# Attention beside an FP4 gated layer on one core: gate, up and down weights handled in portions within the projections, and the main stage's constants and first loads placed in the maximum stage

## The reference

```python
xn = _layernorm(x, axis=-1)
x = x + _L0_attn_ref(xn, Wqkv, Wout, bout) + _L0_ffn_ref(xn, w_gate, w_up, w_down)

# attention: 16 heads of 16, causal
qkv = xn @ Wqkv.T
attn = softmax(where(causal_mask, -inf, q k^T * dh ** -0.5))
out = (attn v) @ Wout.T + bout

# gated layer, width 704; fp4_linear quantises both operands
# in blocks of 16: scale = max|block| / 6, values on a grid of 8
h = silu(fp4_linear(xn, w_gate)) * fp4_linear(xn, w_up)
y = fp4_linear(h, w_down)
```

## Time and profile before

| | |
|---|---|
| median of 3 runs | 2537.82 us (2537.43 to 2541.84) |
| profiled execution | 2539.19 us, span 2537.5 us |
| PE busy | 2314.7 us, 91% |
| DVE busy | 2038.4 us, 80% |
| ACT busy | 1952.0 us, 77% |
| POOL busy | 645.4 us, 25% |
| granted clock of PE, mean | 0.975 of full speed |

### The profile page before, as it was taken

One profiled execution on the slowest core, in us unless ns is written; L12 is line 12 of the kernel. 1 busy time (PEld: TensorE's weight loads), 2 busy tenths in 40 slices (PEclk: granted clock), 3 DMA queues, 4 the chain that ended last, 5 costly groups with the idle time before them and its releaser, 6 DMA issues.

```text
span 2537.5 us, 86209 instructions
## 1 busy us (share of the span) xinstructions
PE 2314.7 (91%) x34104; PEld 1273.9 (50%) x34104; DVE 2038.4 (80%) x5932; ACT 1952.0 (77%) x3342; POOL 645.4 (25%) x524
## 2 busy tenths in 40 slices
PE   2895999999999993999999999999999999999998
PEld 1784444444444441455555555555555555555555
DVE  7674999999999994787777777777777777787775
ACT  1342999999999992888878788878788877788875
POOL 3111343333344322222221222221221221212221
PEclk7898999999999996999999999999999999999999
DMA  2575455545555532111021011021011021011000
GB/s 52 188 225 151 66 76 76 76 71 69 71 69 76 76 52 71 23 31 29 15 68 37 27 40 29 15 68 37 28 40 29 15 68 37 28 39 29 15 21 31
DMA packets 94537, 143.82 MB, mean 57 GB/s; under 512 B 24896, under 2 KB 73920, under 8 KB 93632
## 3 DMA queue, kind: packets, MB, share of 16 engines
q1 hardware_dynamic: 89792, 129.50, 26.1%
q0 software_dynamic: 4352, 8.92, 1.4%
HBM read 104.20 MB, written 34.14 MB: 55 GB/s over the span
## 4 chain that ended last, share of the span: by engine, by line
PE 47%; ACT 7%; issue 5%; DVE 3%; DMA 0%; SPq 0%; POOL 0%; DVEq 0%; ACTq 0%; POOLq 0%
PE O L1051 16%; PE F L1072 10%; PE S L1030 9%; ACT probs L1181 6%; PE F L1109 5%; PE F L1118 2%; PE F L1098 2%; PE S L1036 1%; DVE o_turned L1402 0%; ACT xt_hi L1186 0%; DVE o_turned L1403 0%; PE S L1118 0%; DMA v_in<-s_v 0%; DVE o_sum L1407 0%; DVE xt_lo L1352 0%
## 5 line engine op out<-in xcount | busy, mean ns | idle before, releaser
L1181 ACT ACTIVATE probs<-S 128x1024 f32<-128x1024 f32 (+3 forms) x1280 | 1082.7, 896 | 309.5 <-PE S L1036 184.9
L775 ACT ACTIVATE m_excess<-m_DIFF 128x512 f32<-128x512 f32 (+7 forms) x1536 | 646.8, 472 | 85.7 <-PE m_DIFF L735 40.1
L793 DVE CUSTOM_DVE_ANT_0 m_excess<-m_S,m_excess 128x512 f32<-128x512 f32 (+7 forms) x1536 | 700.6, 530 | 11.7 <-PE m_S L735 9.6
L1051 PE MATMUL O<-probs,v_sb 64*32 64x512 f32 (+3 forms) x10240 | 614.3, 533 | 1.0 <-ACT probs L1181 1.0
L733 PE MATMUL m_S<-m_k,m_q 128*128 128x512 f16 (+7 forms) x1536 | 482.6, 324 | 26.7 <-DVE m_row_max L793 17.4
L733 PE MATMUL m_DIFF<-m_k,m_q_diff 128*128 128x512 f16 (+7 forms) x1536 | 477.6, 318 | 26.6 <-DMA m_q_diff<-s_q 26.3
L1030 PE MATMUL S<-q_st,k_st 64*32 64x512 f16 (+3 forms) x10240 | 414.9, 350 | 82.7 <-ACT probs L1181 43.8
L1030 PEld LDWEIGHTS S<-q_st,k_st 64*32 64x32 f16 x10240 | 148.9, 90 | 412.7 <-ACT probs L1181 251.4
L677 POOL TENSOR_TENSOR m_q_diff<-m_zero,m_q 48x4096 f16<-48x4096 f16 x32 | 224.4, 7011 | 428.8 <-DMA m_q<-s_q 418.1
L733 PEld LDWEIGHTS m_S<-m_k,m_q 128*128 128x128 f16 x1536 | 148.1, 96 | 276.1 <-DVE m_row_max L793 195.5
L735 PE MATMUL m_S<-m_future,m_ident 128*128 128x64 bf16 x1024 | 197.1, 193 | 0.0
(11 more groups left out here) (183 smaller groups left out, 3966.6 us busy)
## 6 DMA issues: line engine op xcount, KB each, us to landing
m_q<-s_q SPq DMA_DIRECT2D x96, 128.0 KB, 3.8
m_k<-s_k SPq DMA_DIRECT2D x96, 128.0 KB, 6.8
m_q_diff<-s_q SPq DMA_DIRECT2D x96, 128.0 KB, 8.1
k_st<-s_k SPq DMA_DIRECT2D x96, 128.0 KB, 4.3
q_st<-s_q SPq DMA_DIRECT2D x384, 32.0 KB
m_k<-s_k SPq DMA_DIRECT2D x96, 124.0 KB, 5.3
a_x<-in_L_attn_x_dram POOLq DMA_DIRECT2D x16, 512.0 KB, 4.8
s_q<-a_part SPq DMA_DIRECT2D x32, 256.0 KB, 2.5
```

Source lines behind the costliest of these rows:

```text
L775: act.activation(excess[u % MAX_EXCESS][:, 0:keys // 2], DIFF[u % MAX_BUFS][:, 0:keys // 2], ACT.Relu) \
L793: dve.tensor_tensor_reduce(larger, S[u % MAX_BUFS][:, 0:keys // 2], larger, 1.0, -3e38, ALU.add, ALU.max, column).then_inc(reduced[u % MAX ...
L1051: ins = pe.matmul(O[e][s * SLOT:(s + 1) * SLOT, st.skip:QC], v_sb[st.group % 2][rows, st.j, s * SLOT:(s + 1) * SLOT], probs[s // 2][st.n % ...
L1181: act.activation(probs[half][st.n % PROBS][:, :, 0:st.width], S[half][:, :, 0:st.width], ACT.Exp, scale=scale).then_inc(exped[half], 1)
```

## The change

The quantisation of the three matrices leaves weights_phase. Their buffers and steps are in a class GatedWeights; weights_phase clears the buffers and issues their loads behind those of Wqkv and Wout. The 16 projection groups are written out without a loop, and at the end of some of them DVE does a portion: all of `scales`, the exponent and step of the rounding, its add, or its subtraction. POOL's `normalise` and `rescale` follow in the same groups. After the last group come the 12 fills, in the banks of the projections. The buffers, constants and first loads of main_phase go to a class Ahead: POOL writes the constants after the first two negations of the maximum stage and places v at its end, SP issues the first loads after the last stacks. The split and store of the last shift (class LastShift) go to the start of POOL's main stage, and a load of queries waits for the store of its own heads' shift. The table of marks gets other numbers.

```diff
+    def clear(self, pool):
+        pool.memset(self.w[0][:, 5 * D:], 0.0).then_inc(self.cleared, 1)
+        pool.memset(self.w[1][:, 5 * D:], 0.0).then_inc(self.cleared, 1)
+        pool.memset(self.w[2][:, :], 0.0).then_inc(self.cleared, 1)
+
+    def load(self, sp, sources):
+        full = (I // P) * P
+        for k in range(2):
+            sp.wait_ge(self.cleared, k + 1)
+            sp.dma_start(self.w[k][:, 0:5 * D].rearrange("p (o k) -> p o k", k=D),
+                         sources[k][0:full, :].rearrange("(o p) k -> p o k", p=P)).then_inc(self.ld[k], 16)
+            sp.dma_start(self.w[k][0:I - full, 5 * D:], sources[k][full:I, :]).then_inc(self.ld[k], 16)
+        sp.wait_ge(self.cleared, 3)
+        sp.dma_start(self.w[2][:, :].rearrange("p (o n) -> p o n", o=KD)[:, :, 0:I],
+                     sources[2].rearrange("(o p) n -> p o n", p=P)).then_inc(self.ld[2], 16)
+
+    def normalise(self, pool, k):
+        pool.wait_ge(self.scaled, k + 1)
+        pool.tensor_tensor(fp4_blocks(self.w[k][:, :]), fp4_blocks(self.w[k][:, :]), per_block(self.rscale[k][:, :], self.nblk),
+                           ALU.mult).then_inc(self.normed, 1)
+
+    def rescale(self, pool, k):
+        pool.wait_ge(self.rounded, k + 1)
+        pool.tensor_tensor(fp4_blocks(self.w[k][:, :]), fp4_blocks(self.w[k][:, :]), per_block(self.scale[k][:, :], self.nblk),
+                           ALU.mult).then_inc(self.quantised, 1)
+
+    def scales(self, dve, k):
+        ch = Chain(dve, self.chain, 3 * k, 3)
+        dve.wait_ge(self.ld[k], 16 if k == 2 else 32)
+        if k:
+            dve.wait_ge(self.scaled, k)
+        ch.tick(dve.tensor_reduce(self.amax[:, :], fp4_blocks(self.w[k][:, :]), AX_X, ALU.max, apply_absolute_value=True))
+        ch.sync()
+        ch.tick(dve.tensor_scalar(self.scale[k][:, :], self.amax[:, :], 1.0 / 6.0, SCALE_MIN, ALU.mult, ALU.max))
+        ch.sync()
+        ch.tick(dve.tensor_scalar(self.rscale[k][:, :], self.scale[k][:, :], NEAR, None, ALU.mult))
+        ch.sync()
+        dve.reciprocal(self.rscale[k][:, :], self.rscale[k][:, :]).then_inc(self.scaled, 1)
+        ch.close()
+
+    def steps(self, dve, k):
+        dve.wait_ge(self.normed, k + 1)
+        if k:
+            dve.wait_ge(self.rounded, k)
+        dve.tensor_scalar(self.step[:, :].bitcast(I32), self.w[k][:, :].bitcast(I32), EXPONENT, None, ALU.bitwise_and) \
+            .then_inc(self.stepped, 1)
+        dve.wait_ge(self.stepped, 3 * k + 1)
+        dve.tensor_scalar(self.step[:, :], self.step[:, :], 1.0, ROUND, ALU.max, ALU.mult).then_inc(self.stepped, 1)
+
+    def add_step(self, dve, k):
+        dve.wait_ge(self.stepped, 3 * k + 2)
+        dve.tensor_tensor(self.w[k][:, :], self.w[k][:, :], self.step[:, :], ALU.add).then_inc(self.stepped, 1)
+
+    def take_step(self, dve, k):
+        dve.wait_ge(self.stepped, 3 * k + 3)
+        dve.tensor_tensor(self.w[k][:, :], self.w[k][:, :], self.step[:, :], ALU.subtract).then_inc(self.rounded, 1)
+
+    def fill(self, pe, f, bank, banks, ident):
+        k, sources, _, _ = self.fills[f]
+        pe.wait_ge(self.quantised, k + 1)
+        if f >= banks:
+            pe.wait_ge(self.lo_made, f - banks + 1)
+        for n, src in enumerate(sources):
+            last = pe.transpose(bank[:, n * P:(n + 1) * P], src, ident[:, :])
+        last.then_inc(self.filled, 1)
+
...
-            pool.wait_ge(identity_made, 2)
-            normalise(0)
-            normalise(1)
-            rescale(0)
-            normalise(2)
-            rescale(1)
-            rescale(2)
+            gated_w.clear(pool)
...
+            sp.dma_start(qkv_in[:, :, :], Wqkv.rearrange("(o p) k -> p o k", p=P)).then_inc(qkv_ld, 16)
...
+            gated_w.load(sp, sources)
...
+SCALES_IN, STEPS_IN, ADD_IN, TAKE_IN = (0, 1, 5), (2, 6, 9), (3, 7, 10), (4, 8, 11)
...
-        def over_groups(eng, body):
-
-            with eng.Fori(0, looped) as r:
-                for p in range(2):
-                    body(r, p, lambda k: True)
-            for g in range(2 * looped, groups):
-                body(g // 2, g % 2, lambda k, g=g: g + k < groups)
+
+        def over_groups(body):
+
+            for g in range(groups):
+                body(g // 2, g % 2, lambda k: g + k < groups)
...
+                g = 2 * r + p
+                if g in TAKE_IN:
+                    gated_w.rescale(pool, TAKE_IN.index(g))
+                if g in SCALES_IN:
+                    gated_w.normalise(pool, SCALES_IN.index(g))
+            over_groups(body)
...
+                g = 2 * r + p
+                if g in SCALES_IN:
+                    gated_w.scales(dve, SCALES_IN.index(g))
+                if g in STEPS_IN:
+                    gated_w.steps(dve, STEPS_IN.index(g))
+                if g in ADD_IN:
+                    gated_w.add_step(dve, ADD_IN.index(g))
+                if g in TAKE_IN:
+                    gated_w.take_step(dve, TAKE_IN.index(g))
+            over_groups(body)
+            for f in range(len(gated_w.fills)):
+                gated_w.low(dve, f, spare[f % len(spare)])
...
+            last = later(0, 0, groups - 1)
+            for f in range(len(gated_w.fills)):
+                if f in (KD, KD + 2):
+                    pe.wait_ge(part1_done[(f - KD) // 2][last[1]], last[0] + 1 + PRIMED)
+                gated_w.fill(pe, f, spare[f % len(spare)], len(spare), ident)
...
+            for f in range(len(gated_w.fills)):
+                gated_w.high(act, f, spare[f % len(spare)])
...
+    def load_first(self, sp):
+        sp.dma_start(self.norm[:, :, :], self.dram["norm"]).then_inc(self.norm_ld, 16)
+        sp.dma_start(self.bias[:, :], self.bout.rearrange("(a n) -> a n", a=1).to_broadcast([P, D])).then_inc(self.bias_ld, 16)
+        self.load_keys(sp, 0)
+        sp.wait_ge(self.q_zeroed, 4)
+        self.load_queries(sp, 0)
+        self.load_values(sp, 0)
+        self.load_tile(sp, 0)
+        self.load_tile(sp, 1)
...
             pool.wait_ge(consts, 6)
             for load in range(2):
                 negate(0, load)
+            ahead.fill(pool, ident)
             for n in range(B * rounds - 1):
...
-            store(B * rounds - 1, loads_before(B * rounds, 0))
+            for p in range(2):
+                pool.wait_ge(q_negated[p], loads_before(B * rounds, 0) + PRIMED)
+            ahead.place_v(pool, 0)
...
                         load_stack(sp, q_diff[p], dram["q"], MAX_Q, head, MAX_LOAD, bass.ds(b * T, T), stack_ld[p])
+            ahead.load_first(sp)
...
-X_TURN_AT = 5
-GATE_AT, UP_AT = (9, 16), (13, 20)
-H_TURN_AT = 31
+X_TURN_AT = 4
+GATE_AT, UP_AT = (9, 16), (13, 22)
+H_TURN_AT = 30
 DOWN_AT = (38, 4)
-X_HIGH_AT, TANH_AT, DECAY_AT, H_HIGH_AT = 5, (19, 20), (14, 19), 33
-X_LOW_AT, COPY_AT, GATED_AT, H_LOW_AT, ADD_DOWN_AT = 8, (9, 17), (18, 29), 34, 7
-X_SCALES_AT, X_ROUND_AT, H_SCALES_AT, H_ROUND_AT = 8, 18, 30, 0
-X_NORM_AT, X_RESCALE_AT, H_NORM_AT, H_RESCALE_AT, BIAS_AT, X_LOAD_AT = 19, 22, 34, 6, 35, 0
+X_HIGH_AT, TANH_AT, DECAY_AT, H_HIGH_AT = 3, (18, 19), (14, 22), 33
+X_LOW_AT, COPY_AT, GATED_AT, H_LOW_AT, ADD_DOWN_AT = 7, (11, 16), (17, 25), 36, 10
+X_SCALES_AT, X_ROUND_AT, H_SCALES_AT, H_ROUND_AT = 10, 17, 32, 0
+X_NORM_AT, X_RESCALE_AT, H_NORM_AT, H_RESCALE_AT, BIAS_AT, X_LOAD_AT = 4, 28, 21, 0, 34, 0
 PROJ_FROM, PROJ_TILES = TILES - 3, 8
 PROJ_AT = ((2,), (9,))
-PROJ_ADD_AT = (2, 15)
+PROJ_ADD_AT = (1, 15)
 HT_SPLIT = 4
 
...
-            pool.wait_ge(bias_ld, 16)
-            place_v(0)
+            last_shift.split(pool, ROUNDS - 1)
             x_normalise(0)
             x_rescale(0)
+            last_shift.store(pool, ROUNDS - 1, dram)
+            pool.wait_ge(bias_ld, 16)
```

More of the change, by code:

```diff
@@ L116, in weights_phase @@
+def weights_phase(nc, sem, wts, gated_w, ident, exp_scale, Wqkv, Wout, sources):
     with ExitStack() as ctx:
@@ L153, in weights_phase @@
-        fills.append(([out_in[:, o, pair * P:(pair + 1) * P] for pair in range(NHG // 2) for o in range(KD)],
-                      (out_ld, 16 * KD * NHG), wts["out"][:, :, :], None))
-        for k, (tile, name) in enumerate(((gate_in, "gate"), (up_in, "up"))):
-            fill_rows(lambda o, kk, tile=tile: tile[:, o * D + kk * P:o * D + (kk + 1) * P], (quantised, k + 1),
-                      wts[name + "_hi"], wts[name + "_lo"])
-        for pair in range(ITILES // 2):
-            fills.append(([down_in[:, o * IPAD + m * P:o * IPAD + (m + 1) * P]
-                           for m in (2 * pair, 2 * pair + 1) for o in range(KD)], (quantised, 3),
-                          wts["down_hi"][:, 2 * pair:2 * pair + 2, :], wts["down_lo"][:, 2 * pair:2 * pair + 2, :]))
@@ L162, in weights_phase @@
-        split = [f for f in range(len(fills)) if fills[f][3] is not None]
-        quant = [w[:, :] for w in (gate_in, up_in, down_in)]
+        fills = [(*f, qk_scaled, 3) for f in fill_rows(lambda o, kk: qkv_in[:, o, kk * P:(kk + 1) * P], wts["qkv_hi"], wts["qkv_lo"])]
```

(11 more changed lines are left out.)

425 lines of the change are left out of this document (200 added, 225 removed).

## The result

The changed kernel takes 2460.27 us in the median of 4 runs, 2538.02 before: 0.9687 of before, 95% interval 0.9672 to 0.9703. That is 78 us less, where I had said 65. The profiled execution has a span of 2460.3 us against 2537.5.

The account below looks back on a forecast made before the run. Inside projections and main stage only PE's time counted; two gaps outside were targeted. From 2537.8 us, -41.7 + 1.0 + 8.0 + 5.5 + 0 - 31.6 - 6.0 = -64.8 gave 2473 us, range 2458 to 2490.

Parts of the forecast that it names:

- The sign: Whole kernel: faster by more than what a measurement can tell (0.2%, 5 us), chance 0.96; slower 0.03.
- both large gains: Earlier end of the weights stage, -41.7 us, and earlier first turn of x at the main stage's entry, net -31.6.
- The weights stage: Kernel start: stage ends with the qkv part at 17.0 instead of 58.68 us; everything after moves by 40.7.
- 1.0 us for a slower landing of x: First x load meets 2 MB of weights under way, 4.8 us may become 6: +1.0 (0 to 2.5).
- The portions: DVE's quantisation work in projection groups, var_eps held some 1.5 us by POOL's multiplication: +8.0 us (1.8 to 12).
- The turns at the end: After projection group 15: 12 fills, ACT's copies of 0.60 us each delay the stage's end: +5.5 us (4.5 to 8.4).
- The maximum stage: POOL's constants and SP's first main-stage loads fit into idle time there: 0 us (0 to +2).
- The entry: Main stage's start: first turn of x 33.1 us earlier, with constants and v's wait gone; net -31.6 (-33.4 to -28).
- The turn ahead of step 1's scores: Main stage's start: these scores, formerly done in waiting time, now follow the turn, costing about 1.5 us.
- The marks: Order of work in main-stage tiles: swap and earlier turn feed PE's 9.8 us wait for xt_lo: -6 us (-25 to +8).
- the one about the marks: Rival, main stage: marks worth much more than 9.8 us since ACT's queue is freer; 2445 us; 5 in 100.
- gives nothing: Projections: writing out the 16 groups instead of looping gains nothing, as PE has no branch-caused idle time there.

Follow-up runs that it names:

- the late turn: Changed kernel with only x_turn and x_high one place later, so scores stand between down products and turn: 2472.45 us, ratio 0.9730.
- halves: Changed kernel with POOL's multiplications of weights cut in halves, one per group, and the portions in other groups: 2457.39 us, ratio 0.9684.

## Why the prediction was right, and where it was off

The sign, both large gains and their causes were right. The time lies at the low end of the range, and nearly all that I had off was off in the same direction. By the steps:

1. **The weights stage** (-40.7 said, -43.0 measured). Right. The last low part comes 1.2 us earlier than reckoned: qkv_in is issued at 0.74 instead of 1.2 and lands the assumed 5.3 us later, and from there it takes 9.8 us, not 10.5. The 1.0 us for a slower landing of x did not come: I had x meet 2 MB of weights under way, and they had all landed by then.
2. **The portions** (+8.0 said). The mechanism is the one I gave, var_eps held by POOL's multiplication, and its size was too large: 0.9 us of hold, not 1.5, since the multiplication took 2.81 here and the 3.39 of the earlier trace rows was itself taken beside DVE; and 1.15 of waiting for each set of scales instead of 2.1. The take portions cost nothing, though var_eps is held 0.9 behind them too. One load of x landed so late that DVE waited 1.17 us for it, 0.5 for PE; of the six other kernels with the same projections one shows this loss and five don't, so it is chance and not a price of the portions. Together 3.9; without portions the stretch from the second group is 4.1 shorter. So the term was about twice too large, and that the stretch comes out near it (+6.6) is luck: it holds two things that my sum didn't have. The clock rose 6.2 us behind the first product instead of 2.9, 1.6 us, and every group is 0.07 us longer.
3. **The turns at the end** (+5.5 said, +3.3 measured). The term was counted wrong: 12 copies of 0.60, 7.2 us, where there are 9 fills. 9 x 0.60 is 5.4, which would have given +3.7. The size of the rest was right.
4. **The maximum stage**: 0 said, +0.2 measured.
5. **The entry**: -33.1 said and measured for the turn. The experiments split it, which my sum did not: loads 15.4, constants 6.5, and 11 left over that I put down to the last shift without a run of its own (x stands last in the queue in these kernels and was second before, so the shares are theirs). The turn ahead of step 1's scores cost 0.7 us and not 1.5: PE's first values start 1.33 us behind the turn in the changed kernel and 0.62 with the late turn.
6. **The marks** (-6 said, -11.2 measured for the whole stretch, for which I had said -4.5). This is the term of the sum that was furthest off. I had written that the stretch "holds at most 68.8 us that another order could give back", PE's idle time, and looked for the gain in its waits for xt_lo. These did halve (9.8 to 4.9), but the waits for ACT rose by as much or more (42.9 to 49.5), so all three rows together went from 57 to 61. What fell was PE's busy time, from 1466.4 to 1449.3. The early turn spares two changes between full and small tiles in 47 of 64 tiles; taken back, it alone brings 10.3 us of busy time and 11 us of the kernel's. That PE's own time depends on the order of its pieces was in none of my rivals; the one about the marks had the direction and named ACT's queue as the reason, which is wrong.

Steps 1, 2, 3 and 6 each came out a little better than I had said, by 2.3, 1.4, 2.2 and 6.7, together 12.6; with the +0.2 of the maximum stage this is the difference of 12.4 between the two traces.

Open is why the changed kernel's products of 512 columns are 233 ns apart where they are 229 before (1.1 us over the stage). It is neither the portions nor the writing out. That the tiles lie elsewhere in memory is left as a reason, and was not tried. Written out, the projections of before measured 3.8 us less (0.0006 to 0.0024 of the time), of which their trace shows only 0.4 within the projections; my "gives nothing" was not right, but the cause of the rest is not found.

## What to carry to other kernels

PE's busy time is not fixed: where it mixes full tiles and small ones, count the changes between them in the order, and try full-tile pieces next to each other if they fall into the same step; but don't empty a step for it: here such steps then waited for ACT. Read the price at each kind of place, for it differed from tile to tile here, and a count times one price only looked right. When work is put beside a multiplication of POOL, list what DVE does in that time by the kind of operation: in this kernel TENSOR_SCALAR from SBUF was held to the end of it however small it was, statistics and subtractions from PSUM were not, so POOL's work is cut to the length of the window that has only the latter. Count the instructions in the order before they become a term of a sum: 12 fills for 9 were 1.8 us of mine. At the border of two stages look for three things separately: what the old stage's end waits for, constants, and the place of the first needed load in its queue.

## What the runs showed of the hardware that I had not expected

- A turn of x between small-tile work costs 0.25 us more of PE than the same turn behind full-tile products (1.13 against 0.88 for the same four pieces), at the 16 tiles whose step has no mask.
- A TENSOR_SCALAR of 128 x 4 elements takes 1.08 us instead of 0.17 while POOL multiplies 128 x 1536, and ends with it; four of 128 x 256 take 2.57 instead of 1.37. The Trainium skill (SBUF — State Buffer, Who interferes with whom) says that the one that comes second is blocked for the whole instruction, and that a Vector instruction with at most one input from SBUF outside its two-port modes does not contend; both agree, the latter with the statistics (1.34 beside POOL's work and 1.41 without).
- The granted clock rose from the 1.2 GHz level to 2.4 GHz 2.9 us behind the first product of the projections in the kernel before and 6.2 behind it in the changed one, with the same work right ahead of it (eight turns, then 2.5 us of nothing). In the seven kernels whose projections are those of the changed one it came 3.6 to 6.2 us behind it, and their first group took from 11.02 to 12.21 us (10.63 to 12.21 over all 14 traces), the longer the later the clock rose. Near the end of the kernel the time at 1.2 GHz differed as well: 6.8 us in the changed kernel, 1.2 in the ones with halves and without portions. Their main stage is the same and takes the same time up to the last tile's turn (1480.8 to 1481.0); behind it they take 40.6 us and the changed kernel 43.5. A difference of 1 to 3 us between two profiles can be this alone.
